# A recommendation tower on one core: another order of the calls on four engines

## The chip, the core and the metric

The kernel runs on one core of a Trainium2 chip. The metric is the device time of one execution in microseconds (us), as the median of the runs shown. Each engine (TensorE for products, VectorE, ScalarE, GpSimd, and SP, which issues most transfers) works through its own list of instructions in order and waits at semaphores for the others.

## The reference: what is computed

For 2048 samples, 39 table rows of 64 numbers are looked up; each row is summed to one number; the products of all pairs of these sums (741) and 16 dense inputs go through three layers.

```python
e = stack([tbl_f[ids[:, f]] for f in range(39)], axis=1)   # 2048 x 39 x 64
s = e.sum(axis=-1)
z = s[:, ROW] * s[:, COL]                                  # all pairs, 741 columns
h = concatenate([z, dense_ctx], axis=1)                    # 757 columns
h = maximum(h @ W_top1 + b_top1, 0)                        # 512
h = maximum(h @ W_top2 + b_top2, 0)                        # 256
y = h @ W_top3                                             # 1
```

20 tables have 1000 rows, 8 have 1250, 8 have 12500 and 3 have 125000.

## The kernel before, in words

**Chunks and tiles.** The batch is cut into 4 chunks of 512 samples; every name below is called with the chunk first, so layer1(2, 3, 1) is chunk 2, rows group 3 of 6, output block 1 of 4.

**Small tables (28 fields, in 7 groups of 4).** The row sums of a whole table are taken once: SP loads a group into one of 4 stage buffers (load_group, L261, over to_stage, L256), VectorE sums it (sum_group, L506) and splits the sums into three bf16 parts (split_groups, L510). An index is split into a shelf and a slot. For each chunk VectorE makes onehots of the shelf (L424) and masks of the slot (L438), TensorE multiplies (lookup, L961), ScalarE copies the result (copy_look, L740), VectorE masks it (pick, L448) and TensorE adds the lanes (sum_lanes, L985). For chunk 0 the indices are spread over the partitions by TensorE (spread, L1046, and spread_slots, L1053) and copied by ScalarE (copy_shelf, L727, and copy_slots, L731); for the later chunks SP stores them in DRAM (save_shelves, save_slots) and loads them back as broadcasts (load_shelves, L284, load_slots, L301, load_mid_shelves, L293). All lookups after chunk 0's go through one PSUM bank, so each waits for the copy of the one before.

**Middle tables.** Four of the tables of 12500 rows are summed like the small ones, in pieces of 33, 33 and 32 columns: SP loads a piece (load_piece, L309), VectorE sums pieces 0 and 1 (sum_piece, L530), and ScalarE sums piece 2 row by row, in four calls of a quarter each (sum_piece, L781). split_middle (L537), mid_onehots, lookup_middle (L998) and pick_middle (L455) do the rest. A stage buffer is loaded again only when its sum is done, and everything behind such a load on SP waits with it.

**Other fields.** GpSimd gathers rows by 128 indirect transfers (L361), in the order of chunks: for each tile 8, 6, 5 or 5 "a" fields, and then the 2 "b" fields of the chunk's four tiles. VectorE sums them (sum_a, L467; sum_b, L473) and splits them (split_a, split_b), TensorE transposes them (transpose_a, L1009; transpose_b, L1017), and ScalarE copies that (place_late_a, place_late_b).

**Pairs and layers.** For each rows group k, TensorE picks both factors with 0/1 matrices (select, L1025), ScalarE copies one (place_factor, L747), VectorE multiplies (multiply, L494), ScalarE rounds (round_z, L751) and VectorE takes the remainder (remainder, L501). select(c, k) waits for the product before it. layer1 (L1064) does three products per block: rounded by rounded, rounded by the weight's remainder, remainder by rounded. Then relu1, remainder_h, layer2 (L1084), relu2, y. The weights are rounded by ScalarE (round_w1, L736) and their remainders taken by VectorE (split_w1, L520).

**What sets the order.** All is written out by hand: one list of calls for each engine, SP at L313 to L351, VectorE at L551 to L718, ScalarE at L819 to L952, TensorE at L1103 to L1283. GpSimd's list (L364 to L375) is a loop and is not touched.

Of the kernel before, what the change touches and what calls it, by code (L numbers as in the profile page):

```python
# [101 lines left out]
def build_tower(nc, ids_rows, ids_cols, dense_t, groups, mid_tables, late_tables, w1, w2, columns, fconst, bconst, out):  # L102
    assert EARLY_PAIRS <= 3 * P and sum(KROWS) == w1.shape[0] and QR_ROWS <= P and max(KROWS) <= P
    with ExitStack() as ctx:
# [147 lines left out]
        def _(sp):  # L252
# [76 lines left out]
            for n in range(1, 4):  # L329
                load_shelves(1, n)  # L330
            save_slots()
            for n in range(3):
                load_piece(2, n)
            load_slots(1)
            load_w2()
            for n in range(4, 6):
                load_shelves(1, n)
            load_mid_shelves(1)
            load_shelves(1, 6)
            load_shelves(2, 0)  # L340
            for n in range(3):
                load_piece(3, n)
            for n in range(1, 7):
                load_shelves(2, n)
            load_slots(2)
            load_shelves(3, 0)
            load_mid_shelves(2)
            for n in range(1, 7):
                load_shelves(3, n)
            load_slots(3)  # L350
            load_mid_shelves(3)  # L351

# [25 lines left out]
        def _(dve):  # L378
# [185 lines left out]
            sum_piece(0, 0)  # L564
            masks(0)
            for n in range(2, 7):
                onehots(0, n)
            sum_piece(0, 1)
            pick(0, 0)
            sum_piece(1, 0)  # L570
            for n in range(2):
                sum_a(0, n)
            pick(0, 1)
            split_middle(0)
            split_w1(0)
            multiply(0, 0)
            split_w1(1)
            mid_onehots(0)
            remainder(0, 0)
            multiply(0, 1)  # L580
            pick_middle(0, 0)
            remainder(0, 1)
            split_w1(2)
            sum_piece(1, 1)
            multiply(0, 2)
            for n in range(2, 4):
                sum_a(0, n)
            split_a(0)
            sum_b(0)
            split_w1(3)  # L590
            remainder(0, 2)
            onehots(1, 0)
            split_b(0)
            for n in range(1, 4):
                onehots(1, n)
            multiply(0, 3)
            for n in range(4, 6):
                split_w1(n)
            remainder(0, 3)
            multiply(0, 4)  # L600
            sum_piece(2, 0)
            remainder(0, 4)
            multiply(0, 5)
            remainder(0, 5)
            sum_piece(2, 1)
            onehots(1, 4)
            split_w2()
            onehots(1, 5)
            mid_onehots(1)
            for n in range(2):  # L610
                remainder_h(0, n)
            onehots(1, 6)
            remainder_h(0, 2)
            masks(1)
            for n in range(2):
                pick(1, n)
            remainder_h(0, 3)
            split_middle(1)
            multiply(1, 0)
            split_middle(2)  # L620
            remainder(1, 0)
            multiply(1, 1)
            pick_middle(1, 0)
            remainder(1, 1)
            sum_a(1, 0)
            pick_middle(1, 1)
            for n in range(1, 4):
                sum_a(1, n)
            pick_middle(1, 2)
            split_a(1)  # L630
            multiply(1, 2)
            onehots(2, 0)
            remainder(1, 2)
            for n in range(1, 3):
                onehots(2, n)
            multiply(1, 3)
            sum_b(1)
            split_b(1)
            remainder(1, 3)
            for n in range(3, 5):  # L640
                onehots(2, n)
            multiply(1, 4)
            onehots(2, 5)
            remainder(1, 4)
            onehots(2, 6)
            sum_a(2, 0)
            multiply(1, 5)
            masks(2)
            pick(2, 0)
            remainder(1, 5)  # L650
            mid_onehots(2)
            pick(2, 1)
            sum_a(2, 1)
            remainder_h(1, 0)
            sum_piece(3, 0)
            for n in range(1, 4):
                remainder_h(1, n)
            multiply(2, 0)
            sum_piece(3, 1)
            remainder(2, 0)  # L660
            multiply(2, 1)
            pick_middle(2, 0)
            sum_a(2, 2)
            remainder(2, 1)
            pick_middle(2, 1)
            split_middle(3)
            pick_middle(2, 2)
            multiply(2, 2)
            sum_a(2, 3)
            pick_middle(2, 3)  # L670
# [50 lines left out]
        def _(act):  # L721
# [108 lines left out]
            for n in range(2):  # L830
                round_w1(n)
# [549 lines left out]
```

## Time and profile before

| what | value |
|---|---|
| median of 3 runs | 198.46 us (198.34 to 200.07) |
| profiled execution: time, span | 198.68 us, 196.9 us |
| busy: TensorE, VectorE, ScalarE, GpSimd | 153.9, 153.9, 120.8, 132.6 us |
| mean granted TensorE clock | 0.913 |
| read from DRAM | 43.37 MB |

The profiled execution is one run; its span reaches from the first to the last instruction, and its own time stands 1.8 us above the span. The profile names an instruction by its line, so that all calls of one helper share a line; which call it is follows from its place in the list.

### The profile page before, as it was taken

The page shows a single profiled execution, that of the slowest core. Times are in us where ns is not written, and L with a number is a line of the kernel's source. Part 1 is how long each engine was busy: PE and PEld are TensorE (multiplying, and loading weights), DVE is VectorE, ACT ScalarE, POOL GpSimd, SP SyncE. Part 2 cuts the span into 40 slices and gives each one's busy share as a digit, 9 for nine tenths or more (in the row PEclk, how much of TensorE's full clock was granted, in tenths as well). Part 3 has the DMA queues.
Part 4 walks back from the last instruction along what each step waited for, and adds up shares of the span by engine and source line. Part 5 has one row for each costly group of instructions (what it writes and reads, how often), then busy time and mean ns, then how long its engine had stood idle before and what let it go on. Part 6 is the DMA issues. An engine that isn't in the chain of part 4 may idle for free.

```text
span 196.9 us, 2964 instructions
## 1 busy us (share of the span) xinstructions
PE 153.9 (78%) x864; PEld 92.7 (47%) x872; DVE 153.9 (78%) x331; ACT 120.8 (61%) x419; POOL 132.6 (67%) x134
## 2 busy tenths in 40 slices
PE   0987500612794989598888999999999999999994
PEld 0212100100571648364665546757656567766781
DVE  1579999997899966998979989998988768534440
ACT  2799900499589879976698476351463746233523
POOL 6777777877777877777777877777778777710000
PEclk9999955555599699999999999999999999999999
DMA  6999999999999999999988399922201111100000
GB/s 185 335 412 417 403 398 406 411 379 325 385 407 401 201 270 378 405 400 389 284 173 262 115 261 324 195 49 80 77 20 30 32 28 24 25 13 3 2 0 0
DMA packets 13696, 43.83 MB, mean 223 GB/s; under 512 B 3628, under 2 KB 4652, under 8 KB 11248
## 3 DMA queue, kind: packets, MB, share of 16 engines
q1 hardware_dynamic: 9048, 39.23, 56.7%
q0 software_dynamic: 4096, 4.20, 9.1%
q10 hardware_dynamic: 536, 0.21, 0.5%
q8 instruction: 7, 0.11, 0.3%
q14 instruction: 9, 0.07, 0.1%
HBM read 43.37 MB, written 0.25 MB: 222 GB/s over the span
## 4 chain that ended last, share of the span: by engine, by line
PE 54%; DVE 20%; ACT 14%; DMA 5%; issue 5%; SPq 1%; ACTq 0%; DVEq 0%
PE ph L1076 13%; PE ph L1080 10%; PE ph L1077 10%; ACT stage L789 9%; DVE tsum L417 7%; DMA stage<-group 5%; PE look L974 3%; DVE msum L417 3%; PE look L1004 2%; PE pa L1035 2%; PE ph L1089 2%; PE ph L1091 2%; PE ph L1090 2%; DVE shelf_b L430 2%; PE pb L1043 2%
## 5 line engine op out<-in xcount | busy, mean ns | idle before, releaser
L361 POOL DMA_INDIRECT rows<-tab,idc x128 | 131.1, 1024 | 39.7 <-issue 38.4
L1076 PE MATMUL ph<-z_hi,w_hi 128*128 128x512 f32 (+2 forms) x96 | 42.9, 447 | 0.0
L1077 PE MATMUL ph<-z_hi,w_lo 128*128 128x512 f32 (+2 forms) x96 | 38.7, 403 | 0.0
L1080 PE MATMUL ph<-z_lo,w_hi 128*128 128x512 f32 (+2 forms) x96 | 38.5, 401 | 0.0
L789 ACT ACTIVATE stage<-stage 128x64 f32<-128x64 f32 x128 | 30.8, 245 | 0.8 <-ACT ids_h L814 0.8
L745 ACT CAST picked<-look 128x512 bf16<-128x512 f32 x25 | 14.9, 594 | 20.5 <-PE look L974 20.3
L498 DVE TENSOR_TENSOR z<-factor,pb 128x512 f32<-128x512 f32 (+2 forms) x24 | 16.4, 684 | 13.7 <-ACT factor L749 13.6
L789 ACT ACTIVATION_READ_ACCUMULATOR stage<-stage 128x1 f32 x128 | 24.3, 190 | 0.0
L759 ACT CAST z_hi<-z 128x512 fp32r<-128x512 f32 (+2 forms) x24 | 14.8, 617 | 13.6 <-DVE z L498 12.6
L974 PE MATMUL look<-shelf_b,tparts 128*32 128x512 bf16 x100 | 10.6, 414 | 15.9 <-DVE shelf_b L430 13.4
L1076 PEld LDWEIGHTS ph<-z_hi,w_hi 128*128 128x128 f32 (+2 forms) x96 | 18.7, 195 | 9.2 <-issue 5.5
L1080 PEld LDWEIGHTS ph<-z_lo,w_hi 128*128 128x128 f32 (+2 forms) x96 | 18.7, 194 | 4.9 <-DVE z_lo L503 0.4
L749 ACT COPY factor<-pa 128x512 f32<-128x512 f32 (+2 forms) x24 | 14.0, 585 | 11.2 <-PE pb L1043 6.8
L503 DVE TENSOR_TENSOR z_lo<-z,z_hi 128x512 fp32r<-128x512 f32 (+2 forms) x24 | 16.5, 687 | 5.5 <-ACT z_hi L759 5.5
L1077 PEld LDWEIGHTS ph<-z_hi,w_lo 128*128 128x128 f32 (+2 forms) x96 | 18.8, 196 | 2.8
L430 DVE TENSOR_SCALAR shelf_b<-shelf_b,fc 128x2048 bf16<-128x2048 bf16 x28 | 20.0, 751 | 0.0
L417 DVE TENSOR_REDUCE tsum<-stage 128x32 f32<-128x2048 f32 (+1 forms) x7 | 16.9, 2431 | 3.3 <-DMA stage<-group 3.3
L417 DVE TENSOR_REDUCE msum<-stage 128x33 f32<-128x2112 f32 x8 | 18.7, 2342 | 0.0
L1050 PE MATMUL ph<-ids_h,bc 128*128 128x512 bf16 x28 | 11.7, 459 | 7.1 <-DVE ids_h L385 5.3
L729 ACT CAST shelf_b<-ph 128x512 bf16<-128x512 f32 x28 | 13.8, 757 | 2.0 <-PE ph L1050 2.0
L1089 PE MATMUL ph<-h,w_hi 128*128 128x512 f32 x32 | 14.3, 448 | 0.0
L974 PEld LDWEIGHTS look<-shelf_b,tparts 128*32 128x32 bf16 x100 | 2.9, 94 | 24.0 <-DVE shelf_b L430 17.2
(82 smaller groups left out, 222.4 us busy)
## 6 DMA issues: line engine op xcount, KB each, us to landing
shelf_b<-shelf_scratch SPq DMA_DIRECT2D x23, 512.0 KB, 9.2
stage<-shelves SPq DMA_DIRECT2D x8, 1056.0 KB, 9.6
stage<-group SPq DMA_DIRECT2D x5, 1024.0 KB, 10.8
stage<-shelves SPq DMA_DIRECT2D x4, 1024.0 KB, 10.0
slot_b<-slot_scratch SPq DMA_DIRECT2D x12, 224.0 KB, 12.1
stage<-group SPq DMA_DIRECT2D x2, 1280.0 KB, 9.0
rows<-tab,idc POOLq DMA_INDIRECT x128, 5.5
w_raw<-w SPq DMA_DIRECT2D x6, 256.0 KB, 7.4
```

What stands on the lines that cost most here:

```text
L361: pool.indirect_dma_start(rows[:, n % ROW_RING, k, :], None, late_tables[k], bass.IndirectOffsetOnAxis(ap=idc[:, at:at + 1], axis=0)).then ...
L417: dve.tensor_reduce(o, stage[:, use % STAGES, 0:n * DIM].rearrange("p (r d) -> p r d", d=DIM), AX.X, ALU.add).then_inc(stage_free[use % ST ...
L430: dve.tensor_scalar(onehot[:, a:b, :], shelf_b[:, a:b, :], fc[:, C_PART:C_PART + 1], None, ALU.is_equal).then_inc(onehot_ready, 1)
L498: dve.tensor_tensor(z[0:KROWS[k], :], factor[0:KROWS[k], :], pb[0:KROWS[k], :], ALU.mult).then_inc(z_product, 1)
L503: dve.tensor_tensor(z_lo[0:KROWS[k], k % ZRING, :], z[0:KROWS[k], :], z_hi[0:KROWS[k], k % ZRING, :].bitcast(F32), ALU.subtract).then_inc( ...
L745: act.copy(picked[:, g, :], bank[:, :]).then_inc(look_copied, 1)
L789: s = act.activation(row, row, ACT.Copy, accum_out=msum[:, i % 2, a + r:a + r + 1])
L974: mm = pe.matmul(bank[lane * LANE:(lane + 1) * LANE, :], tparts[:, f, :], onehot[:, f, :], start=True, stop=True)
L1076: pe.matmul(ph[m][:, :], hi, z_hi[0:n, k % ZRING, :], start=(k == 0), stop=False)
L1077: pe.matmul(ph[m][:, :], lo, z_hi[0:n, k % ZRING, :], start=False, stop=False)
L1080: mm = pe.matmul(ph[m][:, :], hi, z_lo[0:n, k % ZRING, :], start=False, stop=(k == KCH - 1))
L1089: pe.matmul(ph[m][:, :], hi, h1_hi[:, k, :], start=(k == 0), stop=False)
```

## The change: four lists in another order

No helper changes and no call is added or removed; each engine's calls come in another order. The diff, cut to the parts that the prediction speaks of:

```diff
 # SP
-            for n in range(7):
+            for n in range(5):
                 load_group(n)
+            load_w1(0)
+            for n in range(5, 7):
+                load_group(n)
+            load_select()
             load_piece(0, 0)
-            load_select()
+            save_shelves()
             for n in range(1, 3):
                 load_piece(0, n)
             for n in range(2):
                 load_piece(1, n)
-            save_shelves()
-            for n in range(2):
-                load_w1(n)
-            load_piece(1, 2)
             load_mid_shelves(0)
             load_shelves(1, 0)
-            for n in range(2, 6):
+            load_w1(1)
+            load_piece(1, 2)
+            load_shelves(1, 1)
+            for n in range(2, 4):
                 load_w1(n)
...
 # VectorE
             middle_slots()
-            for n in range(2):
-                sum_group(n)
-            for n in range(2):
+            sum_group(0)
+            onehots(0, 0)
+            sum_group(1)
+            for n in range(1, 3):
                 onehots(0, n)
             sum_group(2)
+            onehots(0, 3)
+            sum_group(3)
             split_groups(0)
-            for n in range(3, 5):
-                sum_group(n)
+            sum_a(0, 0)
+            sum_group(4)
+            split_w1(0)
             split_groups(1)
+            onehots(0, 4)
             for n in range(5, 7):
                 sum_group(n)
+            masks(0)
             split_groups(2)
+            pick(0, 0)
+            for n in range(5, 7):
+                onehots(0, n)
+            sum_a(0, 1)
             sum_piece(0, 0)
...
+            sum_a(0, 2)
             sum_piece(0, 1)
...
             pick(0, 1)
+            for n in range(2):
+                sum_piece(1, n)
+            multiply(0, 0)
             split_middle(0)
...
+            remainder(0, 0)
+            sum_a(0, 3)
+            mid_onehots(0)
+            multiply(0, 1)
+            onehots(1, 0)
+            pick_middle(0, 0)
+            onehots(1, 1)
+            split_a(0)
+            remainder(0, 1)
...
             remainder(3, 3)
-            multiply(3, 4)
             sum_b(3)
             split_b(3)
+            multiply(3, 4)
             remainder(3, 4)
...
 # ScalarE
-            for n in range(28):
+            for n in range(19):
+                copy_shelf(n)
+            round_w1(0)
+            for n in range(19, 28):
                 copy_shelf(n)
...
             round_z(0, 0)
             place_factor(0, 1)
+            round_w1(1)
+            sum_piece(1, 2, 0)
             round_z(0, 1)
+            place_factor(0, 2)
+            for n in range(2):
+                copy_look(1, n)
+            place_late_a(0)
             round_w1(2)
...
+            for n in range(2, 4):
+                relu1(0, n)
+            for n in range(4):
+                sum_piece(2, 2, n)
+            for n in range(2):
+                relu2(0, n)
+            copy_look(2, 0)
             place_factor(1, 1)
...
 # TensorE
             for n in range(2):
                 select(0, n)
+            layer1(0, 0, 0)
             lookup_middle(0, 0)
+            layer1(0, 0, 1)
+            select(0, 2)
+            layer1(0, 0, 2)
+            lookup(1, 0)
+            layer1(0, 0, 3)
+            lookup(1, 1)
+            transpose_a(0)
+            layer1(0, 1, 0)
+            select(0, 3)
+            lookup(1, 2)
...
+            lookup(1, 4)
+            select(0, 4)
+            lookup(1, 5)
             transpose_b(0)
...
+            lookup(1, 6)
             layer1(0, 3, 3)
             select(0, 5)
+            sum_lanes(1, 0)
+            layer1(0, 4, 0)
+            sum_lanes(1, 1)
+            layer1(0, 4, 1)
+            select(1, 0)
...
```

Chunks 1 to 3 are rearranged in the same manner: the lookups and lane sums of a chunk stand among layer 1 of the chunk before, on all four lists.

## Rows read from the trace of the kernel before

**Rows 1.** The page, part 1: busy us, share of the span, instructions.
```profile
PE 153.9 (78%) x864; PEld 92.7 (47%) x872; DVE 153.9 (78%) x331; ACT 120.8 (61%) x419; POOL 132.6 (67%) x134
```

**Rows 2.** By stretch: length, TensorE busy (instructions), granted clock, DMA share, GB/s.
```profile
52.40:59.70 7.30, 7.26 (x29) 0.84 1.04 404
59.70:63.50 3.80, 0.98 (x6) 1.00 1.00 401
63.50:80.50 17.00, 16.44 (x73) 0.90 1.05 297
80.50:94.70 14.20, 10.58 (x79) 1.00 1.02 398
94.70:105.00 10.30, 9.03 (x62) 1.00 0.91 209
105.00:185.70 80.70, 79.53 (x472) 1.00 0.34 89
...
65.10:68.40 3.30, 3.30 (x9) 0.50 1.01 210
```

**Rows 3.** VectorE's timeline, front: start, length, line, operation [idle before <- releaser].
```profile
35.27 3.40 DVE L430 TENSOR_SCALAR shelf_b<-shelf_b,fc 128x2048 bf16<-128x2048 bf16 x5
...
41.98 2.34 DVE L417 TENSOR_REDUCE msum<-stage 128x33 f32<-128x2112 f32 x1
...
47.63 0.28 DVE L405 CAST mparts<-msum 128x98 bf16<-128x98 f32 x1 [0.96 <-ACT stage L789]
...
49.80 0.69 DVE L498 TENSOR_TENSOR z<-factor,pb 128x512 f32<-128x512 f32 x1 [0.21 <-ACT factor L749]
```

**Rows 4.** Groups by form, whole span: count | busy us, mean ns | idle before.
```profile
L361 POOL DMA_INDIRECT rows<-tab,idc x128 | 131.1, 1024 | 39.7 <-issue 38.4 <-DMA idc<-ids_cols 1.0 <-DVE a_sum L470 0.3
...
L470 DVE TENSOR_REDUCE a_sum<-rows 128x8 f32<-128x512 f32 x4 | 2.5, 672 | 0.0
```

**Rows 5.** GpSimd's timeline: one fetch beside a pick, and the last one.
```profile
41.03 1.84 POOL L361 DMA_INDIRECT rows<-tab,idc  x1 [0.30 <-issue]
...
171.88 0.94 POOL L361 DMA_INDIRECT rows<-tab,idc  x1 [0.30 <-issue]
```

**Rows 6.** SP's timeline: issue of transfers.
```profile
23.87 10.65 SPq L259 DMA_DIRECT2D stage<-shelves  x4
34.56 0.43 SPq L266 DMA_DIRECT2D shelf_scratch<-ids_h  x1
...
40.95 0.33 SPq L259 DMA_DIRECT2D stage<-shelves  x1
```

**Rows 7.** Stage loads (line 259) issued from 20 to 50 us.
```profile
DMA to landing us min/median/max: 5.8/8.4/10.3
```

**Rows 8.** TensorE's timeline around the first late transpose.
```profile
60.83 0.38 PE L1013 MATMUL early<-bc,a_parts 128*27 128x128 bf16 x4 [1.17 <-DVE a_parts L413]
62.90 0.39 PE L1035 MATMUL pa<-s_early,bc 128*128 128x512 bf16 x1 [1.69 <-ACT s_late L775]
```

**Rows 9.** The chain of waits, 39 to 48 us: start, length, what.
```profile
39.38 5.73 ACT stage L789 x48
```

**Rows 10.** Gathers (line 361) issued from 170 to 175 us.
```profile
DMA to landing us min/median/max: 2.4/2.4/2.5
```

**Rows 11.** VectorE's timeline, tail.
```profile
177.35 0.68 DVE L476 TENSOR_REDUCE b_sum<-rows 128x8 f32<-128x512 f32 x1
...
178.88 0.17 DVE L413 CAST b_parts<-b_rest 128x8 bf16<-128x8 f32 x1
```

**Rows 12.** TensorE's timeline, tail.
```profile
166.91 0.50 PE L1076 MATMUL ph<-z_hi,w_hi 128*128 128x512 f32 x1
...
179.59 0.39 PE L1021 MATMUL early<-bc,b_parts 128*6 128x128 bf16 x4
...
184.42 0.49 PE L1076 MATMUL ph<-z_hi,w_hi 128*128 128x512 f32 x1
```

**Rows 13.** Stage loads (line 259) issued from 50 to 81 us.
```profile
DMA to landing us min/median/max: 10.0/11.5/17.5
```

More of the change, by code:

```diff
@@ L588, in _ @@
[L588 to L621, printed above, removed]
+            remainder(0, 0)
+            sum_a(0, 3)
@@ new lines, in _ @@
+            mid_onehots(0)
[5 more added lines that the diff above has]
+            remainder(0, 1)
+            split_w1(1)
+            multiply(0, 2)
+            onehots(1, 2)
+            split_w1(2)
+            remainder(0, 2)
+            onehots(1, 3)
+            sum_b(0)
+            multiply(0, 3)
+            split_b(0)
+            onehots(1, 4)
+            split_w1(3)
+            remainder(0, 3)
@@ new lines, in _ @@
+            split_w1(4)
+            for n in range(5, 7):
+                onehots(1, n)
+            masks(1)
+            multiply(0, 4)
+            pick(1, 0)
+            split_w1(5)
+            remainder(0, 4)
+            pick(1, 1)
+            sum_piece(2, 0)
+            multiply(0, 5)
+            split_middle(1)
+            remainder(0, 5)
+            split_w2()
+            sum_a(1, 0)
+            multiply(1, 0)
+            sum_a(1, 1)
+            for n in range(3):
+                remainder_h(0, n)
@@ L622, in _ @@
+            mid_onehots(1)
+            sum_piece(2, 1)
+            pick_middle(1, 0)
+            onehots(2, 0)
+            remainder_h(0, 3)
+            onehots(2, 1)
+            pick_middle(1, 1)
+            remainder(1, 0)
+            split_middle(2)
+            for n in range(2, 4):
+                sum_a(1, n)
             multiply(1, 1)
-            pick_middle(1, 0)
+            pick_middle(1, 2)
             remainder(1, 1)
-            sum_a(1, 0)
-            pick_middle(1, 1)
@@ L627, in _ @@
-            for n in range(1, 4):
-                sum_a(1, n)
-            pick_middle(1, 2)
             split_a(1)
+            onehots(2, 2)
             multiply(1, 2)
[L632 to L639, printed above, removed]
             for n in range(3, 5):
                 onehots(2, n)
+            remainder(1, 2)
+            masks(2)
@@ L642, in _ @@
+            onehots(2, 5)
+            multiply(1, 3)
+            onehots(2, 6)
+            sum_b(1)
+            remainder(1, 3)
+            split_b(1)
             multiply(1, 4)
-            onehots(2, 5)
+            sum_piece(3, 0)
             remainder(1, 4)
-            onehots(2, 6)
-            sum_a(2, 0)
+            pick(2, 0)
             multiply(1, 5)
-            masks(2)
-            pick(2, 0)
-            remainder(1, 5)
             mid_onehots(2)
             pick(2, 1)
-            sum_a(2, 1)
@@ L654, in _ @@
-            remainder_h(1, 0)
-            sum_piece(3, 0)
-            for n in range(1, 4):
+            remainder(1, 5)
+            pick_middle(2, 0)
+            sum_piece(3, 1)
+            pick_middle(2, 1)
+            for n in range(2):
                 remainder_h(1, n)
+            onehots(3, 0)
+            remainder_h(1, 2)
             multiply(2, 0)
-            sum_piece(3, 1)
+            pick_middle(2, 2)
+            remainder_h(1, 3)
+            split_middle(3)
             remainder(2, 0)
+            for n in range(2):
+                sum_a(2, n)
@@ L842, in _ @@
+            for n in range(3, 5):
+                round_w1(n)
+            copy_look(1, 3)
             sum_piece(1, 2, 2)
[L843 to L854 removed]
+            copy_look(1, 4)
@@ L1186, in _ @@
-            layer1(1, 5, 0)
-            sum_lanes(2, 1)
-            for n in range(1, 4):
-                layer1(1, 5, n)
-            layer2(1, 0, 0)
-            select(2, 0)
-            lookup_middle(2, 0)
-            layer2(1, 0, 1)
-            layer2(1, 1, 0)
+            lookup(2, 2)
+            for n in range(3):
+                layer1(1, 2, n)
+            lookup(2, 3)
+            layer1(1, 2, 3)
+            select(1, 4)
+            lookup(2, 4)
+            layer1(1, 3, 0)
+            transpose_b(1)
@@ new lines, in _ @@
+            lookup(2, 5)
+            layer1(1, 3, 1)
+            select(1, 5)
+            lookup(2, 6)
+            for n in range(2, 4):
+                layer1(1, 3, n)
+            for n in range(3):
+                layer1(1, 4, n)
+            lookup_middle(2, 0)
+            for n in range(2):
+                sum_lanes(2, n)
+            layer1(1, 4, 3)
+            for n in range(2):
+                layer1(1, 5, n)
+            lookup_middle(2, 1)
+            select(2, 0)
+            for n in range(2, 4):
+                layer1(1, 5, n)
@@ L1217, in _ @@
+            lookup(3, 1)
+            layer1(2, 1, 1)
+            transpose_a(2)
+            for n in range(2, 4):
+                layer1(2, 1, n)
+            select(2, 3)
+            lookup(3, 2)
+            for n in range(3):
                 layer1(2, 2, n)
-            lookup(3, 1)
+            lookup(3, 3)
+            layer1(2, 2, 3)
+            layer1(2, 3, 0)
             select(2, 4)
-            lookup(3, 2)
+            lookup(3, 4)
+            for n in range(1, 3):
+                layer1(2, 3, n)
```

394 lines of the change are left out of this document (162 added, 232 removed).

## The prediction, before the result was known

> **What bounds the kernel now.** I read the page first, then busy time by stretch, then each engine's timeline, and last the gather queue. The page has TensorE and VectorE both at 78%, GpSimd at 67% and ScalarE at 61% [rows 1]; such shares don't say which of them holds the end, the stretches do. From the first layer-1 product (52.4 us) TensorE's list is what the clock runs along. Its idle time in the five stretches is 0.04, 2.82, 0.56, 3.62 and 1.27 us up to 105 us (8.3 in all) and only 1.17 us in the 80.7 us after that [rows 2]. In 65.1 to 68.4 us the granted clock was 0.50 (the 1.2 GHz level), right after the idle stretch 59.7 to 63.5; that is 3.3 us for 1.65 us of work [rows 2]. So about 10 us of TensorE's list before 105 us is stall, and from there it is packed until the last layer 2.
>
> Two other limits matter. Before 49.80 us the bound is VectorE, which goes from one sum to the next [rows 3]. And GpSimd issues one gather each 1.25 us or more to 171.88 us, whatever the others do, since its row shows no wait of weight on them [rows 4, 5].
>
> **The change, part by part.** Nothing is added; every call is moved on its own engine. I walked the four new lists by hand, each step with the duration it has here.
>
> *Front.* The first three sums and four onehots interleave, which fills one wait for a stage load and no more. What stands ahead of multiply(0,0) on VectorE changes by plus one sum_piece (2.34 us long, the next one starts after 2.26), plus one sum_a (0.67), minus split_middle (from 47.63 to 48.90, 1.27: up to 49.80 less the 0.21 of wait and one product of 0.69 like it), minus the waits of 0.96 and 0.21 us that the old order has there, and minus one onehot of 0.67 us that now fills the load wait [rows 3, 4]: multiply(0,0) comes at about 49.6 us instead of 49.80. layer1(0,0,0) can start at 51.2, but lookup_middle(0,0) now follows it instead of leading. Value: 0 to 0.2 us; I take 0. The lookups of groups 2 to 4 leave at about 30 us instead of waiting for the onehots at 35.27 [rows 3], which buys nothing: pick(0,1) still comes at about 44 us behind the sums.
>
> ScalarE now takes round_w1(0) after 19 of the 28 shelf copies. w1's first part is issued at 11 us behind five stage loads and lands near 20, so ScalarE waits about 4.5 us there and its copies end near 29 us. Cover: masks(0) is not due before 33 us. Cost nothing; if that cover were gone, up to 4.5 us.
>
> *SP.* save_shelves moves from 34.56 to about 21 us, which costs nothing and frees the shelf loads later. But SP waits in line at each stage load: sum_piece(0,0) now ends at 41.1 us where the old order had it at 34.1, so load_piece(1,1) goes out at 41.1 and not with the four loads from 23.87, and load_piece(1,2) at 44.1 instead of 40.95 [rows 6]. The queue runs dry for about 2 us before 41 us. sum_piece(1,1) wants its data at 47.2; loads issued in this part landed after 5.8 to 10.3 us [rows 7], so between 46.9 and 51.4. With the queue just emptied I take the short end: no wait. The long end is 4.2 us, kept for the range.
>
> *Chunk 0.* The old stall is at transpose_a(0) and select(0,3): 1.17 us for split_a, then 1.69 us for place_late_a, which queues on ScalarE behind a quarter of sum_piece, round_z and round_w1 and part of another quarter [rows 8]; a quarter is about 1.9 us (24 rows in 5.73) [rows 9]. New: VectorE has split_a(0) before remainder(0,1), ScalarE has place_late_a(0) before round_w1(2), and chunk 1's lookups fill in between. Both waits go, and with them the 1.65 us of the low clock. What is late next: lookup_middle(0,0) waits 0.3 us for mid_onehots(0), lookup(1,5) 0.5 us for copy_look(1,4) behind a quarter sum, and select(1,0), which has been moved into layer 1, 1.45 us for multiply(0,5) behind sum_piece(2,0). Gain of this stage 2.9 + 0.6 + 1.65 - 2.25 = 2.9 us.
>
> *Turn from chunk 0 to 1.* The old 3.62 us [rows 2] are lookups (1,3) to (1,6) handing one bank to and fro, and y(0). New: the lookups are done before; but all four quarters of sum_piece(2,2) stand together on ScalarE, 7.9 us, ahead of relu2(0,0) and round_z(1,1). By my walk they run from 82.4 to 90.3 us while layer 2 runs to 89.7; with 0.65 us for h1_lo and 0.4 for mid_onehots(1) the stalls are 1.95 us. Gain 1.7. From 94.7 to 105, 1.27 us becomes about 1.05. Gain 0.2.
>
> The lead of TensorE's list at 105 us is then 2.9 + 1.7 + 0.2 = 4.8 us. After that there is 1.17 us left to win, and I find no new wait above 0.4 us.
>
> *The cap.* The last gather is issued at 171.88 us and landed after 2.4 us [rows 5, 10], at 174.3. sum_b(3) ran at 177.35, so 3.0 us is all by which it can come earlier. From 174.3: split_b ends 1.7 us later, as before (177.35 to 179.05) [rows 11], at 176.0. transpose_b(3) then still has 5.45 us of TensorE's list before layer1(3,5,0): itself 0.35, two pieces of layer1(3,3) 1.4, select(3,5) 0.95 and layer1(3,4) 2.75, which gives 181.5 us against 184.42 [rows 12]. The lead of 4.8 is cut to 2.9, and 1.9 us shows up as TensorE waiting in front of the late transposes.
>
> Whether 171.88 itself moves is bounded from both sides. 128 fetches took 131.1 us of issue, a mean of 1024 ns; the unhindered ones take 0.94, so 10.3 us were lost [rows 4, 5], as at 41.03 us, where one fetch took 1.84 us beside pick(0,0) [rows 5]. The same bf16 operations run in both orders, so I take no change, and 1.5 us either way for the range. The Trainium skill ("SBUF — State Buffer", Who interferes with whom) says that DMAs issued from GpSimd starve for descriptors while VectorE holds the port pair the two share. The slow fetches agree; by that rule the time depends on which fetch each pick and onehot meets, which is the third rival.
>
> **Sum.** Profiled execution: 198.68 us, span 196.9. Less 2.9 for the cap, plus 0.2 for small waits of the new order: 196.0, span 194.2. The median of the runs is 0.22 lower, at 198.46, so the forecast is 195.8 us.
>
> **Rivals.** *A, a smaller lead.* My walk sums some twenty small waits; if it misses half, or load_piece(1,1) lands at 10.3 us [rows 7] and takes 4.2 of the 4.8, the lead stays near 1 us and the gather does not bind: 198.46 - 1.0 = 197.5. For it: the walk assumes that copies and sums meet as neatly as on paper, and the low clock can come back behind any longer wait, as at 65.1. Against it: the walk leaves 2 us more than the cap needs.
>
> *B, slower: load_piece(1,2) lands late.* ScalarE has sum_piece(1,2,0) now ahead of round_z(0,1), place_factor(0,2) and copy_look(1,0). It comes to it at 52.5 us; the load goes out at 44.1. The six stage loads issued after 50 us landed after 10.0 to 17.5 [rows 13]; here that would be 54.1 to 61.6, a wait of 1.6 to 9.1 us that TensorE meets in full at lookup(1,1), 57.8. The end: 198.46 + 9.1 - 4.8 = 202.8 at worst; it decides from 4.8 us of wait on, a landing later than 13.2 us. For it: DMA is at a share of 1.04 in that stretch [rows 2]. Against it: the six before 50 us took at most 10.3 [rows 7] and fewer bytes are ahead of this one.
>
> *C, the gather moves.* The same price fetch by fetch, but other meetings: 1.5 us earlier or later, 194.3 or 197.3.
>
> **Chances.** Forecast 0.44, A 0.26, B 0.19, C 0.11 (half each way). A measurement of this kernel tells about 1% (2 us) from no change. The forecast's case is 195.2 to 196.4, past the 1% line at 196.5; a tenth of A and half of C fall there too: faster 0.52. Most of A and the late half of C: same 0.29. B: slower 0.19. The range goes from C's early end, 194.3, to 200.0, where A is spent and B's lighter half lies; it leaves out the worse part of B.
>
> **What would show it.** Right: transpose_a(0) and select(0,3) without the 2.9 us; clock at 1.00 from about 57 us on; layer1(3,0) starting 3 to 5 us before 166.91 [rows 12]; TensorE idle 1 to 2 us in all ahead of transpose_a(3) and transpose_b(3), with VectorE waiting at sum_b(3) for the gather; the last gather within 1.5 us of 171.88. Wrong: ScalarE or VectorE waiting for a stage load between 47 and 62 us, or ScalarE's sum_piece(2,2) reaching past 92 us with TensorE idle beside it. Most likely to upset it: landing times, which I carry over from another order of issue.

## The result: 196.88 us, and where the time went

| | before | after |
|---|---|---|
| median of 5 runs each | 199.19 us (198.34 to 200.07) | 196.88 us (196.52 to 197.57) |
| profiled execution: time, span | 198.68, 196.9 us | 197.55, 195.7 us |
| mean granted TensorE clock | 0.913 | 0.904 |

The ratio is 0.9895, 95% interval 0.9849 to 0.9941: faster by about 1%, where 195.8 us was forecast. In a later comparison the same two kernels came to 196.15 and 199.62 us, ratio 0.9824 (0.9785 to 0.9864). Medians here are of all runs and ratios of the fast ones alone (within 1.5% of the fastest of the same kernel), so a ratio need not be the quotient of two medians.

Each trace is one execution. The one of after, 197.55 us, is the second slowest of its five, and the one of before, 198.68 us, lies under its median. These two differ by 1.1 us, the medians by 2.3 us and in the later comparison by 3.5. What follows explains the 1.1 us; where the rest lies no trace shows.

The page of after, part 1, has shares within 1% of those in [rows 1]:

```profile
PE 154.4 (79%) x865; PEld 92.7 (47%) x872; DVE 153.6 (78%) x331; ACT 120.1 (61%) x419; POOL 132.8 (68%) x134
```

So I go to the stretches again. After, nearly the same ones as in [rows 2] (columns: length, then busy us of TensorE, its weight loads, VectorE, ScalarE and GpSimd; granted clock; DMA share; GB/s):

```profile
52.40:59.70 7.30, 6.73 (x44) 4.10 (x43) 7.08 (x22) 6.17 (x24) 5.77 (x6) 0.92 1.04 384
59.70:63.50 3.80, 3.80 (x19) 2.69 (x19) 3.66 (x10) 3.80 (x21) 2.90 (x3) 1.00 1.13 337
63.50:80.50 17.00, 11.01 (x49) 5.63 (x48) 11.14 (x15) 9.28 (x42) 13.15 (x13) 0.81 1.02 298
80.50:94.70 14.20, 13.83 (x72) 9.65 (x70) 12.21 (x27) 11.80 (x61) 10.73 (x12) 0.87 1.04 261
94.70:105.00 10.30, 9.57 (x71) 6.36 (x70) 9.29 (x36) 6.67 (x24) 7.97 (x8) 1.00 1.02 351
105.00:185.00 80.00, 78.84 (x475) 52.44 (x479) 62.45 (x166) 45.37 (x132) 52.66 (x51) 1.00 0.39 115
```

TensorE's idle time in the first five is 0.57, 0, 5.99, 0.37 and 0.73 us, 7.7 in all, against 8.3 before. The 2.82 us at 59.7 is gone; a new block of 6 us stands between 63.5 and 80.5. The same stretch of time holds other work after that: layer 2 of chunk 0, which ran to 92.1 us before, now runs to 96.0, so the turn from chunk 0 to 1 lies across the last two stretches, with 0.37 + 0.73 = 1.1 us idle where it was 3.62 + 1.27. TensorE's timeline of after, from the last product ahead of that block:

```profile
68.62 0.39 PE L1095 MATMUL ph<-z_lo,w_hi 128*128 128x512 f32 x1
74.59 0.62 PE L989 MATMUL look<-shelf_b,tparts 128*32 128x512 bf16 x4 [5.58 <-issue]
...
97.08 0.47 PE L1091 MATMUL ph<-z_hi,w_hi 128*128 128x512 f32 x1 [0.72 <-ACT h L820]
```

Line 989 at 74.59 is lookup(1,6). The row blames "issue", that is, nothing that the profile shows; the other engines' timelines tell more. ScalarE, then VectorE, of after:

```profile
73.39 0.62 ACT L753 CAST w_hi<-w_raw 128x512 fp32r<-128x512 f32 x1 [5.98 <-DMA w_raw<-w]
...
96.26 1.25 ACT L820 ACTIVATE h<-ph,cols 128x512 f32<-128x512 f32 x2
```

```profile
68.17 0.75 DVE L438 TENSOR_SCALAR shelf_b<-shelf_b,fc 128x2048 bf16<-128x2048 bf16 x1 [2.05 <-DMA shelf_b<-shelf_scratch]
...
72.73 1.28 DVE L453 TENSOR_SCALAR slot_b<-slot_b,fc 128x2560 bf16<-128x2560 bf16 x2 [3.81 <-DMA slot_b<-slot_scratch]
```

ScalarE stands at round_w1(5) until w1's last part has landed, with copy_look(1,5) queued behind it, and lookup(1,6) needs the bank which that copy frees. VectorE waits beside it, for the last shelves and for the slots of chunk 1. All three transfers are late. (The last row of ScalarE is relu2(0,0), which comes directly behind sum_piece(2,2).) SP's list of after:

```profile
24.79 16.06 SPq L259 DMA_DIRECT2D stage<-shelves  x4
...
43.38 0.33 SPq L259 DMA_DIRECT2D stage<-shelves  x1
...
47.16 3.22 SPq L271 DMA_DIRECT2D slot_scratch<-ids_h  x4
...
60.98 1.73 SPq L305 DMA_DIRECT2D slot_b<-slot_scratch  x4
62.75 0.42 SPq L279 DMA_DIRECT2D w_raw<-w  x1
```

The transfers as a whole, after, by stretch; the second-last column is the DMA share:

```profile
36.00:47.00 11.00, 2.91 (x16) 0.60 (x17) 11.00 (x10) 8.88 (x64) 8.56 (x9) 0.50 0.70 247
62.00:71.00 9.00, 6.98 (x39) 4.55 (x35) 4.74 (x11) 5.30 (x24) 6.87 (x8) 1.00 1.06 207
75.00:80.00 5.00, 4.62 (x16) 2.06 (x13) 5.00 (x5) 4.03 (x20) 4.09 (x4) 0.50 1.02 405
80.00:85.00 5.00, 5.00 (x15) 3.01 (x15) 3.01 (x9) 3.15 (x5) 3.78 (x5) 0.57 1.02 386
```

and the same two stretches of the kernel before:

```profile
36.00:47.00 11.00, 3.90 (x27) 0.93 (x27) 10.50 (x11) 9.96 (x66) 8.56 (x9) 0.50 0.99 369
62.00:71.00 9.00, 8.07 (x35) 4.70 (x35) 6.88 (x16) 7.52 (x30) 6.87 (x8) 0.81 1.04 242
```

Three things are to be seen. From 36 to 47 us the queue of after runs low, because SP stands in the block of 16.06 us at its stage loads (load_piece(1,1), the fourth, goes out at 40.52): 0.30 x 11 = 3.3 us of transfer time are not used. From 62 to 71 us it is full and only 207 GB/s arrive. And behind the stall of TensorE the granted clock is 0.50 (the 1.2 GHz level) to 80 us and 0.57 in the mean from 80 to 85, that is, at that level until about 84 us and at 1.00 after it: some 9.4 us, against 3.3 before [rows 2].

The tail of after, TensorE:

```profile
165.81 0.50 PE L1091 MATMUL ph<-z_hi,w_hi 128*128 128x512 f32 x1
...
169.92 0.38 PE L1028 MATMUL early<-bc,a_parts 128*27 128x128 bf16 x4 [0.41 <-DVE a_parts L421]
...
178.15 0.39 PE L1036 MATMUL early<-bc,b_parts 128*6 128x128 bf16 x4
```

VectorE's sum_b(3), and GpSimd's last gather:

```profile
175.14 0.68 DVE L484 TENSOR_REDUCE b_sum<-rows 128x8 f32<-128x512 f32 x1
```

```profile
172.06 0.94 POOL L369 DMA_INDIRECT rows<-tab,idc  x1 [0.30 <-issue]
```

Layer 1 of chunk 3 starts 1.10 us before 166.91 and transpose_b(3) 1.44 us before 179.59 [rows 12]. sum_b(3) waits for nothing. So in these two traces the lead of TensorE's list is about 1 us, not 4.8, and the gather does not hold the end. Nearly all of that lead was there before layer 1 began: select(0,1) starts at 49.38 us after and at 50.55 before, 1.17 us apart. From there to layer1(3,0) the new lists win nothing net.

### The profile page after: what moved, and what is told of

The parts are those of the page before. It is cut to its first block, busy times and chain, and to the rows that moved or that the text cites. A ratio compares the mean times of both kernels' runs of the same rounds, so it can differ in the third digit from the quotient of the medians.

```text
span 195.7 us, 2965 instructions
## 1 busy us (share of the span) xinstructions
PE 154.4 (79%) x865; PEld 92.7 (47%) x872; DVE 153.6 (78%) x331; ACT 120.1 (61%) x419; POOL 132.8 (68%) x134
## 4 chain that ended last, share of the span: by engine, by line
PE 56%; DVE 22%; issue 7%; ACT 7%; DMA 5%; SPq 1%; ACTq 1%; DVEq 0%
PE ph L1091 13%; PE ph L1092 10%; PE ph L1095 10%; DVE tsum L425 7%; DMA stage<-group 5%; ACT stage L804 4%; DVE msum L425 4%; PE look L989 3%; PE ph L1104 3%; PE ph L1106 3%; PE ph L1105 3%; PE look L1019 3%; DVE shelf_b L438 2%; PE pb L1058 2%; DVE a_sum L478 2%
## 5 line engine op out<-in xcount | busy, mean ns | idle before, releaser
L1091 PE MATMUL ph<-z_hi,w_hi 128*128 128x512 f32 (+2 forms) x96 | 44.2, 461 | 1.3 <-ACT h L820 0.7
L438 DVE TENSOR_SCALAR shelf_b<-shelf_b,fc 128x2048 bf16<-128x2048 bf16 x28 | 20.9, 758 | 2.0 <-DMA shelf_b<-shelf_scratch 2.0
L470 DVE SCALAR_TENSOR_TENSOR mid_picked<-bc,mid_slot,look 128x98 f32<-128x98 bf16 x48 | 12.3, 312 | 2.9 <-PE look L1019 2.8
L1104 PE MATMUL ph<-h,w_hi 128*128 128x512 f32 x32 | 13.5, 423 | 0.1
## 6 DMA issues: line engine op xcount, KB each, us to landing
w_raw<-w SPq DMA_DIRECT2D x6, 256.0 KB, 11.2
```

The lines of the kernel that those rows point to most:

```text
L438: dve.tensor_scalar(onehot[:, a:b, :], shelf_b[:, a:b, :], fc[:, C_PART:C_PART + 1], None, ALU.is_equal).then_inc(onehot_ready, 1)
L1091: pe.matmul(ph[m][:, :], hi, z_hi[0:n, k % ZRING, :], start=(k == 0), stop=False)
L1104: pe.matmul(ph[m][:, :], hi, h1_hi[:, k, :], start=(k == 0), stop=False)
```

## Experiments

Two sets of runs fell on an occasion when every kernel took half as long again (the kernel before 315.01 and 315.35 us), because from about 35 to 105 us TensorE's spreading of the slots and ScalarE's copies of them came only about once in 10 to 11 us, and VectorE waited for them (more in the last section). Their ratios stand here, but they say little of an undisturbed run; the questions that mattered were asked again. The others had the kernel before at 199.57 (early_slots_b, fewer_gathers_b) and 199.62 us (changed_again to w1_last_early).

**Was it SP's wait for the slot store?** SP issues load_slots(1) only at 60.98 us, after a wait of 9.0 us for save_slots to land, and load_w1(5) behind it.

```diff
 load_piece(0, 0)
 save_shelves()
+save_slots()
 ...
 load_w1(4)
-save_slots()
```

> The changed kernel with one call of SP moved: save_slots() directly behind save_shelves(), at about 21 us instead of 47 us. Theory S (the lead was lost at SP's wait of 9.0 us for the slot store, which held back load_slots(1) and load_w1(5)): the TensorE wait of 5.6 us at lookup(1,6) near 69 to 74 us and the low clock behind it (8 us at 0.50, worth 4 us) go. If the gather then caps the end, as the prediction says (last issue 172.06 + 2.4 us, TensorE waiting at transpose_b(3)), the time is 195.0 to 196.2 us, some 1 to 2 us under the changed kernel's 196.9; without a cap it would be 187 to 190 us. Rival D (the transfers themselves are the limit in that stretch, whatever SP waits for): the slots and w1's last part land no earlier than 71 us and the time stays at 196.5 to 197.5 us.

> The same kernel as early_slots, on another occasion: there every kernel, the one before too, stood still for some 80 us after 35 us, with TensorE's and ScalarE's next instruction 10 us apart, so the stretch in question could not be read. Expectations as there. Theory S: the 5.6 us of TensorE at lookup(1,6) and the low clock behind it go; with the gather's cap 195.0 to 196.2 us, without a cap 187 to 190. Rival D: the slots and w1's last part land no earlier than 71 us, 196.5 to 197.5 us.

Measured: 300.8 us, ratio 0.9604 (0.9459 to 0.9749), in the disturbed set; 196.1 us, ratio 0.9813 (0.9762 to 0.9864), in the other. Of early_slots_b, SP, ScalarE and TensorE:

```profile
50.22 2.44 SPq L305 DMA_DIRECT2D slot_b<-slot_scratch  x4
52.71 0.42 SPq L279 DMA_DIRECT2D w_raw<-w  x1
```

```profile
72.98 0.62 ACT L753 CAST w_hi<-w_raw 128x512 fp32r<-128x512 f32 x1 [5.76 <-DMA w_raw<-w]
```

```profile
74.18 0.62 PE L989 MATMUL look<-shelf_b,tparts 128*32 128x512 bf16 x4 [5.31 <-issue]
```

Slots and weights are issued some 10 us earlier and land at the same time (the slots 18.9 to 20.4 us behind their issue, against 8.3 to 10.3 in after); the stall shrinks by 0.27 us. The time lies in theory S's range, but so does that of the changed kernel itself, 196.15 us in the next set, and the stall that S says should go is there. SP's wait is not the cause. What is issued earlier stands longer in the queue.

**Only the weight part ahead of the slot store.**

```diff
 load_w1(4)
+load_w1(5)
 save_slots()
 ...
 load_slots(1)
-load_w1(5)
```

> The changed kernel with load_w1(5) ahead of save_slots() instead of behind load_slots(1); the slots stay as they are. It parts the two waits of that stretch: ScalarE's 5.98 us for w1's last part, VectorE's 3.81 us for the slots. If the w1 wait alone holds TensorE, lookup(1,6) comes 5 us earlier but layer1(0,3,3) and select(0,5) then meet the slots' wait (multiply(0,4) behind masks(1), and place_late_b(0) behind round_z(0,4)): theory S expects 196.0 to 197.2 us, a gain of no more than 1 us. Rival W (w1's late part is the whole cause): the 5.6 us go and the gather caps the end, 195 to 196 us.

Measured in the disturbed set alone: 300.46 us, ratio 0.9657 (0.9539 to 0.9775). Nothing follows; w1_last_early below asks the same.

**Does the gather hold the end?** In chunk 3, six of the eight gathers of b fields are left out, so the last b sums are other numbers; all else is the changed kernel.

```diff
-for t in range(TILES):
+for t in range(TILES if c < CHUNKS - 1 else 1):
     for k in range(NA, NL):
```

> The changed kernel with 6 of the 8 b gathers of chunk 3 left out (tiles 1 to 3; sum_b(3) sums what stands in the ring there). The last gather is issued some 7.5 us earlier, near 164.6 us. Theory T (the changed kernel's end is set by TensorE's list, packed from 175 us on, and the gather is done 0.7 us before it is asked for): no change, 196.4 to 197.4 us. Rival G (the prediction's cap): sum_b(3) comes earlier and the end with it, 194 to 195.5 us.

> The same kernel as fewer_gathers, on another occasion, for the same reason: the changed kernel with 6 of the 8 b gathers of chunk 3 left out. Theory T (TensorE's list sets the end of the changed kernel): no change, 196.4 to 197.4 us. Rival G (the prediction's cap): 194 to 195.5 us.

Measured: 297.64 us, ratio 0.9548 (0.9422 to 0.9675), disturbed; 196.13 us, ratio 0.9805 (0.9756 to 0.9854), with the same kernel before (199.57 us) as early_slots_b; the changed kernel itself came to 196.15 us, ratio 0.9824, in the next set. fewer_gathers_b, its last gather and its sum_b(3):

```profile
165.34 0.95 POOL L369 DMA_INDIRECT rows<-tab,idc  x1 [0.30 <-issue]
```

```profile
174.59 0.68 DVE L484 TENSOR_REDUCE b_sum<-rows 128x8 f32<-128x512 f32 x1
```

The last gather is issued 6.7 us sooner than in after, while sum_b(3) comes only 0.55 us sooner, and layer1(3,0), which does not depend on these gathers, comes 0.50 sooner too (165.31 us, 165.81 in after). The time is a little under theory T's range, as that of the changed kernel itself is. In the changed kernel the end is TensorE's list. The margin is small: 172.06 + 2.4 us of landing is 0.7 us ahead of the 175.14 of sum_b(3).

**The SP list alone.** The kernel before with the changed kernel's SP list.

> The kernel before with only SP's list in the new order; VectorE, ScalarE and TensorE keep the old lists. Theory S: the new SP list by itself costs, since it sends the slot store behind more loads and w1's last part behind the slots: round_w1(4), round_w1(5) wait on ScalarE in front of place_late_b(0); 200 to 205 us against 198.5 to 199.2. Rival: the SP list is neutral and the other three lists alone bring the gain and the new stall; 198 to 199.5 us.

> The kernel before with the changed kernel's SP list alone; the lists of VectorE, ScalarE, TensorE and GpSimd are the old ones. Theory L (the engines' lists bring the gain, by taking lookup(1,5) and its neighbours away from loads that had not landed): 199.0 to 200.5 us, no faster than before. Rival Q (the order of the loads brings it): 196 to 197 us. TensorE's idle spell at 59.7 to 63.5 us and the low clock behind it should still be there under L and be gone under Q. The prediction said nothing of this half by itself; its own working puts the 2.9 us of chunk 0 on the list of TensorE, so it stands with L.

Measured, both times in a disturbed set: 316.1 us, ratio 1.0108 (1.0035 to 1.018), and 317.69 us, ratio 1.0174 (1.007 to 1.0278). Next to it each kernel with the new lists of the engines had a ratio of 0.95 to 0.97. That speaks for the lists of the engines as the source of the gain (both intervals of the SP list alone lie above 1), but a stop of some 75 us stands in every one of these runs, and on an undisturbed chip it was not measured.

**The changed kernel again**, on the chip of the next three:

> The changed kernel itself, beside the others of this comparison, as their base: 196.5 to 197.6 us, a ratio of 0.985 to 0.994 to the kernel before. early_slots_b had slots land at 72.6 us although they were issued 10.8 us earlier, so theory S is out for the stall. New theory Q: the transfers are the limit. SP holds everything behind load_piece(1,1) from 33 to 40.5 us, the transfer queue runs low from 37 to 47 us (229, 260 and 263 GB/s), and those 1.7 MB are missing 25 us later, when shelves(1,6), the slots and w1(5) land 2 to 6 us after they are asked for.

Measured: 196.15 us, ratio 0.9824 (0.9785 to 0.9864), a little under what was expected. lookup(1,6) starts at 75.05 after 4.99 us of idle time; the stall is there again.

**Fill the gap in the queue.** All that needs no free stage buffer goes ahead of load_piece(1,1), at which SP stands.

```diff
 load_piece(0, 0)
 save_shelves()
+save_slots()
 for n in range(1, 3):
     load_piece(0, n)
-for n in range(2):
-    load_piece(1, n)
+load_piece(1, 0)
+for n in range(1, 6):
+    load_w1(n)
 load_mid_shelves(0)
 load_shelves(1, 0)
-load_w1(1)
+load_piece(1, 1)
 load_piece(1, 2)
...
 load_slots(1)
-load_w1(5)
```

> The changed kernel with SP's list altered in one place: save_slots() at 21 us, and w1(1) to w1(5), load_mid_shelves(0) and load_shelves(1,0) ahead of load_piece(1,1), so that 1.95 MB fill the queue while SP waits for sum_piece(0,0). Theory Q: slots(1) land near 68 us instead of 72.7, no wait for w1(5); TensorE's stall of 5.6 us near lookup(1,6) falls to 0.5 to 1.5 us and the low clock behind it goes (4 us): lead up by 7 to 8 us at 90 us. Then the gather's cap of the prediction binds: span 193.9 to 194.4, time 195.5 to 196.0, TensorE idle 3 us or more between 165 and 180 us. If there is no cap: 188 to 191 us. Rival: load_piece(1,1) now lands late (after 46.4 us) and the front is lost by as much as the stall wins: 196.5 to 198 us.

> fill_gap with 6 of the 8 b gathers of chunk 3 left out (sum_b(3) sums what stands in the ring for tiles 1 to 3), so the last gather is issued 7.5 us earlier. If the gather caps fill_gap, this one is faster by 1 to 4 us, 191.5 to 194.5; a(3,3)'s gather, issued at about 161 us, is the next cap. If TensorE's list sets fill_gap's end, the two are equal within 0.4 us.

Measured: fill_gap 197.11 us (194.39 to 197.58; five of the six runs lie at 196.7 or above), ratio 0.981 (0.975 to 0.9869); with the six gathers left out as well 193.9 us (193.3 to 195.51), ratio 0.9719 (0.9674 to 0.9764). The time of fill_gap missed theory Q's 195.5 to 196.0 and lies in the rival's range; the trace shows how much of each came true. fill_gap by stretch, and its TensorE:

```profile
36.00:47.00 11.00, 2.91 (x16) 0.60 (x17) 10.62 (x9) 8.74 (x63) 8.56 (x9) 0.50 1.04 390
...
75.00:80.00 5.00, 4.02 (x18) 2.53 (x19) 4.65 (x9) 4.48 (x12) 3.77 (x4) 1.00 1.02 392
80.00:85.00 5.00, 4.21 (x17) 2.43 (x16) 5.00 (x9) 3.57 (x14) 3.81 (x4) 1.00 1.09 259
```

```profile
52.30 0.61 PE L1044 MATMUL pa<-s_early,bc 128*128 128x512 bf16 x1 [5.47 <-DVE z L500]
...
71.98 0.40 PE L983 MATMUL look<-shelf_b,tparts 128*32 128x512 bf16 x4
...
101.20 0.39 PE L1052 MATMUL pb<-s_late,bc 27*128 27x512 bf16 x1 [0.16 <-issue]
...
161.95 0.50 PE L1085 MATMUL ph<-z_hi,w_hi 128*128 128x512 f32 x1
...
167.76 0.38 PE L1022 MATMUL early<-bc,a_parts 128*27 128x128 bf16 x4 [2.12 <-DVE a_parts L415]
...
177.93 0.38 PE L1030 MATMUL early<-bc,b_parts 128*6 128x128 bf16 x4 [1.85 <-DVE b_parts L415]
```

The queue is full (390 GB/s in place of 247), lookup(1,6) runs at 71.98 without a wait, and the clock stays at 1.00. The slots, issued at 46.80 us behind the same loads as in early_slots_b and w1's last part as well, landed after 17.7 to 19.0 us, by about 67 us, where they landed at 72.6 in early_slots_b. That points to the filled queue, and not to their place in it, as what brings them early. The price is ahead of it: VectorE now waits 2.68 us for a stage load at 49.30, so this select starts 2.9 us later than the 49.38 of after. Even so the product at 101.20 comes 4.5 us before its twin of after (105.70), and layer1(3,0) at 161.95 comes 3.9 us before the one of after and 4.96 us before 166.91 [rows 12]. Then the gather takes it back. VectorE and GpSimd of fill_gap:

```profile
176.07 0.69 DVE L478 TENSOR_REDUCE b_sum<-rows 128x8 f32<-128x512 f32 x1 [2.98 <-DMA rows<-tab,idc]
```

```profile
173.62 0.94 POOL L363 DMA_INDIRECT rows<-tab,idc  x1 [0.30 <-issue]
```

The last "a" sum, sum_a(3,3), waits as well, 1.39 us for its rows. TensorE idles 2.12 + 1.85 = 3.97 us ahead of the late transposes. With fewer gathers the second wait is gone and the first is halved:

```profile
166.23 0.38 PE L1022 MATMUL early<-bc,a_parts 128*27 128x128 bf16 x4 [1.11 <-DVE a_parts L415]
```

transpose_a(3) comes 1.53 us earlier and the second wait, 1.85 us, is gone; together that is the 3.4 us by which the spans of the two traces differ (195.5 to 192.1; the intervals of the two ratios just touch). Only the second part is the doing of the six gathers: the last a gather was issued at 162.06 us here and at 163.20 in fill_gap, with nothing left out ahead of either. Both parts are waits for the gather, so with the lead there, the gather is the cap.

**Only w1's last part ahead of load_piece(1,1).**

```diff
 load_piece(1, 0)
+load_w1(5)
 load_piece(1, 1)
 ...
 load_slots(1)
-load_w1(5)
```

> The changed kernel with load_w1(5) alone moved, ahead of load_piece(1,1) at about 33 us; the slots stay. It parts the two late transfers. If ScalarE's 6.0 us for w1(5), which stands ahead of copy_look(1,5), is what holds TensorE: lookup(1,6) no longer waits, but select(0,5) meets multiply(0,4), which waits for the slots until 72 us. Theory Q (both are late because of the queue, and the slots' lateness is nearly as great): gain at most 1 us, 195.9 to 197.2. Rival W (w1(5) alone): 195 to 195.8 us with the stall gone.

Measured: 196.76 us, ratio 0.9842 (0.9808 to 0.9876), inside theory Q's range. Its VectorE and TensorE:

```profile
71.80 1.28 DVE L453 TENSOR_SCALAR slot_b<-slot_b,fc 128x2560 bf16<-128x2560 bf16 x2 [3.63 <-DMA slot_b<-slot_scratch]
...
176.02 0.69 DVE L484 TENSOR_REDUCE b_sum<-rows 128x8 f32<-128x512 f32 x1 [2.26 <-DMA rows<-tab,idc]
```

```profile
75.86 0.60 PE L1052 MATMUL pa<-s_late,bc 38*128 38x512 bf16 x1 [5.16 <-DVE w_lo L530]
```

ScalarE's wait is gone and lookup(1,6) runs at 69.41, but VectorE has multiply(0,4) behind masks(1), which wait for the slots. ScalarE's round_z(0,4) waits for that product until 73.71 (4.88 us), with place_late_b(0) queued behind it, and that ends at 75.42, when select(0,5) can start. (The row names split_w1(5), which ended in the same moment.) The stall has moved and stays 5.16 us long. Two waits stood in parallel, and taking one away shows the other. Something was won all the same: layer1(3,0) starts at 164.21 us, 1.6 us before the one of after. The gather took it back: its last issue was at 173.59 us, sum_b(3) waits 2.26 us for it, and TensorE 0.53 + 1.13 us ahead of the late transposes. With a lead of 2.7 us over the kernel before, the cap already binds.

**Are the slot loads slow themselves?** The slot loads of chunk 1 bring one group of seven.

```diff
-def load_slots(c):
+def load_slots(c, n=GROUPS):
 ...
-        sp.dma_start(slot_b[lane * LANE:(lane + 1) * LANE, :, :],
-                     slot_dram[lane, c].rearrange("g n -> (g n)")...
+        sp.dma_start(slot_b[lane * LANE:(lane + 1) * LANE, 0:n, :],
+                     slot_dram[lane, c, 0:n].rearrange("g n -> (g n)")...
```

> The changed kernel with the slot loads of chunk 1 cut from seven groups a lane to one (128 KB instead of 896 KB in all); the masks of the other six groups are made from what the buffer holds, so the sums of chunk 1 are other numbers, and the work of all engines is the same. Theory W (the slot loads themselves hold the queue: while they move, all 16 DMA engines are busy and only about 200 GB/s arrive): the window 65:71 us shows over 330 GB/s, the slots have landed by 69 us and w1(5) by 70, lookup(1,6) starts by 70.5 instead of 74.59, the clock stays at 1.00 until 85 us, and the run takes 194.5 to 196.2 us with a wait for the gather of 1 to 2.5 us before transpose_b(3), as in the kernel that filled the gap. Rival V (the queue is simply behind, whatever moves): 768 KB less at 390 GB/s brings w1(5) 2.0 us earlier, lookup(1,6) at 72.6, the low clock stays, and the time is that of the changed kernel within 0.5 us.

Measured in a disturbed set: 298.48 us, ratio 0.9534 (0.9435 to 0.9632). Its time settles nothing, nor does the stall, since instructions were held up there too. The transfer rate can be read, beside fewer_gathers, which has the same SP list and suffered the same stop. one_slot_group (slot loads issued at 139.5 us), then fewer_gathers (139.0 us):

```profile
143.00:146.00 3.00, 3.00 (x8) 2.32 (x8) 2.86 (x9) 3.00 (x19) 1.30 (x2) 0.50 1.05 392
146.00:149.00 3.00, 3.00 (x14) 1.67 (x13) 3.00 (x6) 2.36 (x12) 2.39 (x3) 0.73 1.03 392
```

```profile
143.00:146.00 3.00, 3.00 (x17) 2.04 (x16) 2.86 (x9) 3.00 (x16) 1.89 (x2) 1.00 1.01 210
146.00:149.00 3.00, 2.78 (x14) 1.46 (x12) 2.99 (x5) 2.29 (x17) 2.11 (x3) 1.00 0.99 280
```

With the slot loads cut the queue moves 392 GB/s at a share of 1.05; with them whole 210 GB/s at a share of 1.01. Their landing took 3.6 to 4.4 us against 7.5. So theory W holds as to the rate; how much of the stall it is worth was not measured.

## Why the prediction was right, and what in it was wrong

The forecast of 195.8 us lies 1.1 us under the median, and the range held. Its ratio to the 198.46 us of before, 0.9866, lies between the two measured, 0.9895 and 0.9824. The class is open: 196.88 us is on the "same" side of the 196.5 us that the text drew, the ratio 0.9895 just on the other side of 1%, with the line inside its interval. The way there was another, so that the closeness is in part luck: no lead of 4.8 us and no cap that takes 1.9 of it, but what rival A described, a lead near 1 us, with the end on TensorE's list and, as rival A also named, the low clock back behind a longer wait. Of the signs listed for "right", only the missing 2.9 us and the time of the last gather came.

*Front.* Taken as 0, walked to 49.6 us; multiply(0,0) came at 48.66 with no wait at the stage loads, 1.1 us before 49.80 [rows 3]. Of the 0.9 us that the walk lacks, 0.69 is split_w1(0): before it stood at 48.90, right ahead of this product, and after it runs at 24.68; the walk does not take it off. The short end for sum_piece(1,1) was right, and so was the cover of ScalarE's wait for w1(0), 5.46 us against 4.5.

*Chunk 0.* The 2.9 us of stall [rows 8] are gone as forecast, and the clock at 65 us is 1.00. (The 0.6 in that sum has no source in the text; the idle time of 0.56 us in the stretch from 63.50 [rows 2] is of that size.) The new waits were put at 2.25 us; the one that counts was not among them: 5.58 us at lookup(1,6). With it the low clock came back, for about 9.4 us (74.6 to 84) in place of 3.3, at half the full clock 4.7 us of work lost in place of 1.65.

*Turn.* From 80.50 to 105 us TensorE idled 1.1 us where 1.95 + 1.05 were walked. sum_piece(2,2) did hold TensorE up, though by less than feared: it ran on ScalarE from 88.61 to 96.26 us (the walk had 82.4 to 90.3), and the first product of layer1(1,0) stood 0.72 us at 97.08 for the relu2 behind it. TensorE itself came some 6 us later than in the walk, which hid the rest.

*The failed step* is "the lead of TensorE's list at 105 us is then 4.8 us". It was about 1.1 us, read at layer1(3,0) in the two traces, and even between the medians no more than 2.3 to 3.5 us lie. The terms that make it up, 2.9 + 1.7 + 0.2 from chunk 0 on, came to nothing net, and the front, put at 0, brought the 1.1. The mis-sized term is the 2.25 us of new waits: 5.58 us of stall and the longer low clock were missing in it. The cause lies one part earlier: the text saw that "the queue runs dry for about 2 us before 41 us" and priced this only at the next stage load. Measured, it was 3.3 us of unused transfer time, and the bytes not moved then were missing at the end of the backlog, at the shelves, slots and weights due at 66 to 73 us. fill_gap shows it: with that time used, TensorE stands 4.5 us further on at 101 us than in the changed kernel, and 4.96 us ahead of before at layer1(3,0), which is the lead that was forecast, with 2.9 us lost at its front; the stall and the low clock are both gone. Of the three late transfers none alone is the cause (early_slots_b, w1_last_early).

*The second oversight* was in front of me. [rows 2] has 210 GB/s at a share of 1.01 beside 404 at 1.04. I read the share as "busy" and not the rate. The four slot loads write 32 partitions each. By the Trainium skill ("SBUF — State Buffer", Door 1: The DMA port swizzle) a transfer's rate depends on how many of 16 ports its partitions reach, and 32 partitions reach 8, half of them. The trace agrees: 210 GB/s with the loads whole, 392 with them cut, and 207 in the changed kernel from 62 to 71 us. That the ports are the mechanism was not tested by itself.

*The cap.* Not reached in the changed kernel, and right where it is: in fill_gap sum_b(3) waits 2.98 us for the gather, and transpose_b(3) follows 1.86 us behind it (1.7 was reckoned from landing). TensorE waited 3.97 us there, not 1.9, with the last gather issued 1.7 us later than the 171.88 us reckoned with, and with the gather of the last "a" fields late as well, which the text did not price (2.12 of the 3.97 us). The 5.45 us of list from transpose_b(3) to layer1(3,5,0) was right: 5.52 in after (178.15 to 183.67).

*Rival B* did not come: load_piece(1,2) went out at 43.38 and ScalarE waited 0.89 us for it at 52.44. The danger named, a late landing on a moved queue, was real, but for loads further back. *Rival C* is of the size given: the last gather was issued at 172.06 and 170.99 us in two runs of the same program, and at 173.62 in fill_gap; its mean stayed at 1017 to 1038 ns against 1024 [rows 4]. In neither trace of the changed kernel did it set the end, but with 0.7 us to spare in after, a last issue at 173.6, as in fill_gap and w1_last_early, would have. The example that stands beside the page's rule in the prediction does not fit it: the fetch of 1.84 us stands beside pick(0,0), a tensor_tensor, and the same section of the Trainium skill ("SBUF — State Buffer", Who interferes with whom) names tensor_tensor as an operation that did not stall such transfers. The measurement decides; the sum does not rest on the rule.

What stays open: the share of the SP list in the gain on an undisturbed chip, and a version that keeps fill_gap's lead. fill_gap is no faster than the changed kernel (0.981 and 0.9824, intervals overlapping), and in its trace the gather takes what the queue gives; 193.9 us is what it would be worth with six gathers fewer.

## What to carry to other kernels

When one queue carries all loads, a spell in which it runs low may be paid for by the last loads of the backlog, as here, and not by the next one; so price a moved blocking load by the queue's unused time and look for who waits at its far end. Read share and rate together: a full share at half the rate marks transfers to be moved, reshaped or counted double. And before crediting a lead, find every transfer due in that stretch, for waits that stand in parallel only show one at a time.

## What the runs showed of the hardware that was not expected

- On two occasions every kernel that ran was slowed in the same place. TensorE's timeline of old_lists_new_sp_b, spreading the slots, then GpSimd's:

```profile
59.43 0.62 PE L1067 MATMUL ph<-ids_h,bc 128*32 128x512 bf16 x4 [10.58 <-issue]
70.63 0.62 PE L1067 MATMUL ph<-ids_h,bc 128*32 128x512 bf16 x4 [10.58 <-issue]
```

```profile
59.90 0.94 POOL L369 DMA_INDIRECT rows<-tab,idc  x1 [0.30 <-issue]
```

The products take 0.62 us and stand 11.2 us apart, waiting for nothing that the profile shows. ScalarE's copies of the slots stand as far apart (58.70, 69.90, 81.10), and VectorE waits 66.84 us for them. GpSimd goes on with a gather each 1.25 us. The kernel before was as slow there (315 us), but left no trace of it. The cause is not known.

- A low clock follows the stall and outlasts it: idle from 69.0 to 74.6 us, then a clock of 0.50 until about 84 us although TensorE was busy 4.62 of 5.00 us and then all the time.
